# A transformer block on one core: the attention's residual moves from VectorE to TensorE and ScalarE

## The chip, the cores and the metric

The kernel runs on one core of a Trainium2 chip. The metric is the device time of one execution in microseconds (us), as the median of several runs. All five engines of the core work side by side, each through its own list of instructions in the order in which they are written; semaphores join them.

## The reference, cut to what matters

The input x has the shape (2, 128 channels, 128, 128). Two residual blocks follow each other.

```python
x = x + attention(ln_c(x))        # shifted 8x8 windows, 8 heads, then a 128x128 projection Wproj and bproj
t = tokens(x)                     # 32768 tokens of 128 channels
t = t + ffn(ln_t(t))              # graph attention over 524288 edges gives gates for 4 experts
```

Inside the attention the last two steps are `einsum('oc,bchw->bohw', Wproj, out) + bproj`, and then the sum with the x that came in. That sum with x, the first residual, is what the change moves. Everything is float32. The graph part needs the edges sorted by their destination.

## The kernel before

**Stages.** The program has three stages. The first (to about 1937 us) computes the attention and, on VectorE in the time that is left there, sorts the 524288 edges with a network of compare-and-exchange steps. The second (to about 7400 us) gathers rows for the sorted edges with GpSimd's indirect DMAs, while the experts are computed. The third joins the gates and the experts. The change is in the first stage.

**Strips and rounds.** The image is cut into 32 strips of 8 rows (1024 tokens, 16 windows). A loop of 34 rounds runs a pipeline over them: round t normalizes strip t (`has_m`), makes scores and exponentials of strip t-1 (`has_n`), and weighs, projects, adds the residual to and normalizes strip t-2 (`has_c`). So the residual is added in rounds 2 to 33, once per strip, in two halves j of 4 rows (512 tokens) each.

**Banks.** PSUM's banks 6 and 7 are used by turns: use u of a round lies in bank 6 + u % 2. TensorE raises `full[u % 2]` when a use is written, and the engine that copies it out raises `evac[u % 2]`; `free(u)` makes TensorE wait for the copy of the use before. Uses 6 and 7 are the two halves of the projection, uses 8 and 9 the centering of the sum x1 for the second normalization.

**The order on each engine in one round**, as far as it touches the change, with the lines of the profile:

- VectorE (`round_dve`): weigh window group 0 (L648); add biases and take maxima for the scores of group 0 (L628, L636, L639); a slot of sort steps (L420, L421); weigh group 1 (L648), which completes `ot`; a slot of sort steps; **the residual, four `scalar_tensor_tensor` (L665, L667)**; the scores of group 1 (L628, L633, L636, L639); two more slots of sort steps.
- TensorE (`round_pe`): attend to group 0 (L769, L785, L791), scores of group 0 (L805), center x (L746), attend to group 1, two means (L750), **the projection, halves 0 and 1 (L841)**, the scores of group 1 (L805), the centering of x1 (L746), values (L864), two means (L750), queries and keys (L884), the node rows (L895).
- ScalarE (`round_act`): copies of PSUM for the attention (L926), inverse sums (L934, L936), exponentials (L963), the log and inverse square root of the variance (L950, L956), the square and copy of the centered x1 (L942, L943), the values (L996), log and inverse root again, queries and keys (L1010 to L1016), exponentials (L963), node rows (L1026).
- SyncE stores x1, x2 and the node rows of a strip, and loads the strip after next but one into the same `xt` when uses 6 and 7 have been copied out.

The projection needs both weighed groups: TensorE waits with the second mean and the projection until VectorE has written `ot` for group 1. The scores of group 1 on VectorE need TensorE's L805 for group 1, which stands behind the projection in TensorE's list.

**The sort and its turns.** From round 8 on, each level of the sort takes three rounds. The steps across partitions need the keys turned by TensorE. In the first round of a level (8, 11, ... 29; called A here) VectorE asks for a turn after its third slot, and TensorE turns 8 pieces at the end of its round (L715), with ScalarE copying them out (L910). In the second round (9, 12, ... 30; B) VectorE asks for the turn back after its second slot, and TensorE turns 8 pieces between the values, after it centered x1 (L715, L907). In the third round (10, 13, ... 31; C) there is no turn. Rounds 2 to 7 have only sort steps, and rounds 32 and 33 end the pipeline. A constant `ident`, the 128x128 identity that the transposes use as well, lies in SBUF.

Of the kernel before, what the change touches and what calls it, by code (L numbers as in the profile page):

```python
# [11 lines left out]
ALU = mybir.AluOpType  # L12
ACT = mybir.ActivationFunctionType
# [4 lines left out]
IMGS, H, W = 2, 128, 128  # L18
M = IMGS * H * W
NH, DK, WS, SS = 8, 16, 8, 4  # L20
# [126 lines left out]
OPEN = 4  # L147
# [16 lines left out]
def program(nc, x, wq_t, bq, wkv_t, bkv, wproj_t, bproj, bias_table, w_gat, att_src, att_dst, b_gat, ln_gamma,  # L164
# [9 lines left out]
    with ExitStack() as ctx:  # L174
        scopes = [ctx]

        def sb(name, shape, dt=F32):
            return scopes[-1].enter_context(nc.sbuf_tensor(name, shape, dt))

        def sem(name):  # L180
            return ctx.enter_context(nc.semaphore(name))

        bank = ctx.enter_context(nc.psum_tensor("bank", [P, 8, 512], F32))
        cst = sb("cst", [P, CONST_COLS])

        def con(name):
            return cst[:, CONST[name][0]:CONST[name][1]]
# [4 lines left out]
        vec = sb("vec", [C, 9])  # L192
# [19 lines left out]
        evac = [sem(f"evac{b}") for b in range(2)]  # L212
        full = [sem(f"full{b}") for b in range(2)]
# [11 lines left out]
        strip_saved = sem("strip_saved")  # L225
# [71 lines left out]
        bias = sb("bias", [P, 4, NH // 2, L])  # L297
# [20 lines left out]
        xt = [a.rearrange("c (i w) -> c i w", w=W) for a in parts[:UNROLL]]  # L318
# [11 lines left out]
        x1 = [sb(f"x1{b}", [C, WS, W]) for b in range(UNROLL)]  # L330
# [270 lines left out]
        def pass_over(e, semaphore, before, n):  # L601

            e.wait_ge(semaphore, before + OPEN)
            e.sem_inc(semaphore, n)

        def has(t):

            return 0 <= t < STRIPS, 0 <= t - 1 < STRIPS, 0 <= t - 2 < STRIPS

        def round_dve(e, t, d, own):  # L610
            _, has_n, has_c = has(t)
            par = (t - 2) % UNROLL

            def scores(g):
                if not has_n:
                    pass_over(e, biased, t * 3 + g, 1 + g)
                    pass_over(e, centered, t * 2 + g, 1)
                    return
                e.wait_ge(s_full, t * 2 + g + 1 + OPEN)

                e.wait_ge(pt_full[1], pt_uses(t, g, 1) + 2 + OPEN)
                kind = 2 * ((t - 1) % 16 // 15)

                sums = bank[:, 0:4, :].rearrange("p (a b) (w x) -> p a (b w) x", a=2, w=4)
                taken = prob[g][:, :, :, :].rearrange("p w (a b) s -> p a w (b s)", a=2)
                biases = bias[:, :].rearrange("p k (a b) s -> p a k (b s)", a=2)
                n = 8 - g
                e.tensor_tensor(taken[:, :, 0:n], sums[:, :, 0:n],  # L628
                                biases[:, :, kind:kind + 1].broadcast_to([P, 2, n, 2 * L]),
                                ALU.add).then_inc(biased, 1)  # L630
                if g:

                    e.tensor_tensor(taken[:, :, n:8], sums[:, :, n:8], biases[:, :, kind + 1:kind + 2],  # L633
                                    ALU.add).then_inc(biased, 1)
                e.wait_ge(biased, t * 3 + 1 + 2 * g + OPEN)
                own.step(e.tensor_reduce(row_max[:, g], prob[g][:, :, :, :], AX, ALU.max))  # L636
                own.settle()
                pr = prob[g][:, :, :, :].rearrange("p w h s -> p (w h) s")
                e.tensor_tensor(pr, pr, row_max[:, g].rearrange("p w h -> p (w h)").unsqueeze(2)  # L639
                                .broadcast_to([P, 32, L]), ALU.subtract).then_inc(centered, 1)  # L640

            def weigh_attention(g, u):
                if not has_c:
                    return

                wait_full(e, t, u)
                e.wait_ge(sums_turned, t * 2 + g + 1 + OPEN)
                e.tensor_tensor(ot[:, 8 * g:8 * g + 8].rearrange("p w i j -> p (w i j)"), bank[:, 6 + u % 2, :],  # L648
                                inv[g][:, :], ALU.mult).then_inc(evac[u % 2], 1)

            weigh_attention(0, 0)
            scores(0)
            if t:
                sort_slot(d, t, 0)
            weigh_attention(1, 3)
            sort_slot(d, t, 1)
            if has_c:
                for j in range(2):

                    wait_full(e, t, 6 + j)  # L660
                    e.wait_ge(strip_saved, t - 3 + OPEN)
                    pr = bank[:, 6 + j, :].rearrange("p (i c) -> p i c", c=W)
                    rws = slice(4 * j, 4 * j + 4)
                    old = xt[par]
                    e.scalar_tensor_tensor(x1[par][:, rws, SS:W], pr[:, :, 0:W - SS], vec[:, 6:7],  # L665
                                           old[:, rws, SS:W], ALU.add, ALU.add)
                    e.scalar_tensor_tensor(x1[par][:, rws, 0:SS], pr[:, :, W - SS:W], vec[:, 6:7],  # L667
                                           old[:, rws, 0:SS], ALU.add, ALU.add).then_inc(evac[j], 1)
            scores(1)
            sort_slot(d, t, 2)  # L670
            sort_slot(d, t, 3)


        def pt_uses(t, g, b):

            each = 3 - b
            return t * (2 * each) + each * g

        def wait_evac(e, t, u):
            e.wait_ge(evac[u % 2], t * USES + u // 2 + 1 + OPEN)  # L680

        def wait_full(e, t, u):
            e.wait_ge(full[u % 2], t * USES + u // 2 + 1 + OPEN)
# [41 lines left out]
        def round_pe(e, t, k, strips, loads, turns=0, across=None, back=None):  # L725
# [3 lines left out]
            has_m, has_n, has_c = strips  # L729
            now, before, last = k, (k - 1) % UNROLL, (k - 2) % UNROLL  # L730

            def free(u):

                e.wait_ge(evac[u % 2], t * USES + u // 2 + OPEN)

            def skip(u):

                free(u)
                e.sem_inc(full[u % 2], 1)
                e.sem_inc(evac[u % 2], 1)  # L740

            def bk(u):
                return bank[:, 6 + u % 2, :]
# [90 lines left out]
            for j in range(2):  # L834
                if has_c:
                    if j == 0:

                        wait_evac(e, t, 0)
                        wait_evac(e, t, 3)
                    free(6 + j)  # L840
                    e.matmul(bk(6 + j), wproj_s[:, :],  # L841
                             ot[:, :, 4 * j:4 * j + 4, :].rearrange("c w i j -> c i w j"),
                             start=True, stop=True).then_inc(full[j], 1)
                else:
                    skip(6 + j)
            score(1)
# [7 lines left out]
            for g in range(2):  # L854
                if has_n:
                    free(10 + g)
                    for w in range(8):
# [4 lines left out]
                        for half in range(2):  # L862
# [3 lines left out]
                                         start=True, stop=True)  # L866
# [12 lines left out]
            for g in range(2):  # L879
                for n, wgt in enumerate((wq_s[:, :], wkv_s[:, 0:C])):  # L880
                    u = 14 + 2 * g + n
                    if has_m:
                        free(u)
                        e.matmul(bk(u), wgt, xw[now][:, 8 * g:8 * g + 8].rearrange("c w i j -> c (w i j)"),  # L884
                                 start=True, stop=True).then_inc(full[n], 1)
# [4 lines left out]
            for j in range(2):  # L890
                if has_c:
                    e.wait_ge(xn_done, t * 4 + 3 + j + OPEN)
                    free(18 + j)
                    for r in range(4):
                        m = e.matmul(bank[:, 6 + j, ROW * r:ROW * r + ROW], x2[last][:, 4 * j + r, :], wgat_s[:, :],  # L895
                                     start=True, stop=True)
# [19 lines left out]
        def round_act(e, t, k, strips, turns=0, across=False, back=False):  # L916
            has_m, has_n, has_c = strips
            last = (k - 2) % UNROLL
# [19 lines left out]
            def centered_copy(n, u0):  # L938
                for j in range(2):
                    u = u0 + j  # L940
                    wait_full(e, t, u)
                    e.activation(sq[n][:, j], bank[:, 6 + u % 2, :], ACT.Square)  # L942
                    e.activation(xc[n][:, j], bank[:, 6 + u % 2, :], ACT.Copy).then_inc(evac[u % 2], 1)  # L943
# [34 lines left out]
            else:  # L978
                pass_over(e, rstd_ready, t * 4, 2)
            if has_c:  # L980

                e.wait_ge(xn_done, t * 4 + OPEN)
                centered_copy(1, 8)
            if has_n:
                for g in range(2):
# [3 lines left out]
                    for half in range(2):  # L989

                        rws = slice(64 * half, 64 * half + 64)
# [610 lines left out]
        def _(e):  # L1602
# [11 lines left out]
            for t in range(ROUNDS):  # L1614
                round_dve(e, t, d, own)
# [29 lines left out]
        def _(e):  # L1645
# [3 lines left out]
            for t in range(FIRST_ALL):  # L1649
                if t == 1:  # L1650

                    e.wait_ge(setup_done, 1)
                round_pe(e, t, t, has(t), 1)
            with e.Fori(0, (FIRST_TURN - FIRST_ALL) // UNROLL) as i:
                for k in range(FIRST_ALL, FIRST_ALL + UNROLL):
                    round_pe(e, i * UNROLL + k, k % UNROLL, (True,) * 3, i + k // UNROLL + 1)
            with e.Fori(0, LEVELS // 2) as i:
                for level in range(2):
                    turns = i * 4 + 2 * level

                    for k, keyed in enumerate((dict(across=key(0)), dict(back=key(1 - level)), {})):
                        t = FIRST_TURN + UNROLL * level + k
                        round_pe(e, i * (2 * UNROLL) + t, t % UNROLL, (True,) * 3, i * 2 + t // UNROLL + 1,
                                 turns + k, **keyed)
# [286 lines left out]
```

## Time and profile before

| | |
|---|---|
| median of 3 runs | 8058.88 us (8057.36 to 8060.34) |
| the profiled execution, its own time | 8058.64 us |
| its span in the profile | 8056.8 us |
| busy in the span: TensorE, VectorE, ScalarE, GpSimd | 3009.5, 3627.7, 1934.5, 4712.0 us |
| mean granted TensorE clock | 0.666 |

A share of busy time over the whole span says little here, since the stages have different limits: in the second stage GpSimd is busy three quarters of the time, in the first VectorE and TensorE about four fifths each. The change has to be judged inside the first stage, by what each engine waits for in a round. A line like `L841 MATMUL ... x4` stands for two float32 matmuls: the chip's list has two passes for each, and each pass has a weight load of its own.

### The profile page before, as it was taken

Reading aid. Unit: us, or ns where it says so; the run is one execution under the profiler, and the core shown is the slowest. Engines: PE = TensorE matmul, PEld = TensorE weight load, DVE = VectorE, ACT = ScalarE, POOL = GpSimd, SP = SyncE. Lnnn points to the kernel's source line nnn. Section 1 sums busy time; section 2 is a strip of 40 time slices with the busy share of each in tenths; the row PEclk is TensorE's granted clock in tenths of the full one; section 3 lists DMA queues with packets and bytes.
Section 4 is the critical chain, followed back from the end, with each engine's and each line's share of the span. In section 5 each row is a group of like instructions: output and inputs, shape, how many; then the busy total and the mean of one; then the engine's idle time right before and its main releaser. Section 6 shows DMA issues by size and latency. Waiting matters only on the chain.

```text
span 8056.8 us, 48889 instructions
## 1 busy us (share of the span) xinstructions
PE 3009.5 (37%) x14746; PEld 1474.1 (18%) x14746; DVE 3627.7 (45%) x3863; ACT 1934.5 (24%) x2929; POOL 4712.0 (58%) x4876
## 2 busy tenths in 40 slices
PE   3678887775122222222222212221212121200678
PEld 2345544442000100000001100000000000000222
DVE  5997788885323332333233324321211111111799
ACT  1446665552112121212121212121111111100000
POOL 1111121114777777777777777777777777776641
PEclk9889999897565666666666656665656565655555
DMA  1001111011122222222222222221111111111455
GB/s 52 26 26 34 34 34 34 29 32 57 45 70 57 70 65 62 57 70 69 58 57 70 71 56 57 70 54 31 41 31 41 31 41 31 39 18 46 137 184 173
DMA packets 284782, 455.39 MB, mean 57 GB/s; under 512 B 121214, under 2 KB 204382, under 8 KB 262366
## 3 DMA queue, kind: packets, MB, share of 16 engines
q1 hardware_dynamic: 134760, 395.08, 13.4%
q0 software_dynamic: 147648, 56.99, 6.4%
q8 instruction: 111, 1.82, 0.1%
q10 hardware_dynamic: 2208, 1.05, 0.1%
q14 instruction: 55, 0.45, 0.0%
HBM read 231.36 MB, written 221.42 MB: 56 GB/s over the span
## 4 chain that ended last, share of the span: by engine, by line
POOL 52%; issue 20%; DVE 3%; PE 1%; DMA 1%; POOLq 0%; ACT 0%; DVEq 0%
POOL gath L1319 51%; PE bank L1561 1%; DVE yo L1534 1%; POOL got L1596 1%; DMA gate_rows<-gate_dram 0%; DMA gate_dram<-turned_gates 0%; DVE fin L1539 0%; DVE s L1495 0%; DVE sc L1470 0%; POOL first L1749 0%; DVE s L1468 0%; DMA got<-edge_rows,end_i 0%; DVE sc L1482 0%; DVE sc L1489 0%; DVE sc L1474 0%
## 5 line engine op out<-in xcount | busy, mean ns | idle before, releaser
L1319 POOL DMA_INDIRECT gath<-node_rows,idx x4352 | 4125.3, 948 | 1326.3 <-issue 1326.3
L1272 PE MATMUL bank<-xm,w_s 128*128 128x512 f32 x1024 | 640.7, 770 | 3744.5 <-ACT scratch_i L1293 3732.3
L1228 DVE TENSOR_TENSOR adst_in<-bank,gath 128x256 f32<-128x256 f32 x68 | 53.4, 786 | 2819.5 <-DMA gath<-node_rows,idx 2819.5
L1272 PEld LDWEIGHTS bank<-xm,w_s 128*128 128x128 f32 x1024 | 227.4, 241 | 4142.8 <-ACT scratch_i L1293 3999.3
L1300 ACT ACTIVATE bank<-diff 128x256 f32<-128x256 f32 x68 | 26.3, 387 | 3740.4 <-DVE diff L1245 3740.4
L1046 POOL TENSOR_TENSOR scratch_i<-xc,dst_f 128x480 f32<-128x480 f32 x64 | 121.1, 1892 | 1128.6 <-ACT dst_f L956 1128.6
L1279 PE MATMUL bank<-scratch_i,w_s 128*128 128x512 f32 x1024 | 540.1, 685 | 195.7 <-ACT scratch_i L1293 118.5
L1215 DVE TENSOR_SCALAR scratch_i<-bank,b_s 128x512 f32<-128x512 f32 x256 | 190.4, 750 | 917.6 <-PE bank L1279 522.4
L1561 PE MATMUL bank<-gate_rows,choose 4*128 4x512 f32 x512 | 447.4, 1065 | 62.1 <-DVE yo L1534 50.5
L1293 ACT ACTIVATE scratch_i<-bank,b_s 128x512 f32<-128x512 f32 x512 | 345.1, 683 | 187.6 <-PE bank L1272 186.8
L1596 POOL DMA_INDIRECT got<-edge_rows,end_i x256 | 245.3, 958 | 208.3 <-DVE gates L1522 130.6
L1057 POOL TENSOR_TENSOR x<-xc,dst_f 128x512 f32<-128x512 f32 x64 | 159.5, 2510 | 354.0 <-ACT dst_f L956 354.0
L1310 ACT ACTIVATE rows<-sums 128x1280 f32<-128x1280 f32 x68 | 230.4, 3388 | 390.2 <-DVE sums L1256 390.2
L1279 PEld LDWEIGHTS bank<-scratch_i,w_s 128*128 128x128 f32 x1024 | 217.4, 220 | 522.2 <-issue 420.2
L1539 DVE TENSOR_REDUCE fin<-yo 128x512 f32<-128x2560 f32 x64 | 288.0, 4500 | 4.3
L420 DVE TENSOR_TENSOR key_a<-key_b 128x1024 f32<-128x1024 f32 (+1 forms) x144 | 266.6, 1852 | 2.3
L421 DVE TENSOR_TENSOR key_b<-key_a 128x1024 f32<-128x1024 f32 (+1 forms) x139 | 258.3, 1858 | 0.0
L420 DVE TENSOR_TENSOR key_b<-key_a 128x1024 f32<-128x1024 f32 (+1 forms) x139 | 244.7, 1760 | 29.4 <-ACT key_a L907 27.3
L421 DVE TENSOR_TENSOR key_a<-key_b 128x1024 f32<-128x1024 f32 (+1 forms) x144 | 253.3, 1759 | 0.0
L1561 PEld LDWEIGHTS bank<-gate_rows,choose 4*128 4x128 f32 x512 | 163.8, 328 | 335.4 <-issue 233.6
L791 PE MATMUL bank<-pt,vb 128*64 128x64 f32 x4096 | 210.5, 250 | 31.7 <-ACT pt L926 31.0
L1250 DVE TENSOR_TENSOR terms<-bank,gath 128x1024 f32<-128x1024 f32 x68 | 182.2, 2679 | 63.5 <-ACT weight L1302 63.5
(216 smaller groups left out, 5650.0 us busy)
## 6 DMA issues: line engine op xcount, KB each, us to landing
gath<-node_rows,idx POOLq DMA_INDIRECT x4352
y_dram<-scratch_i SPq DMA_DIRECT2D x64, 1024.0 KB, 4.0
yo<-y_dram SPq DMA_DIRECT2D x64, 1024.0 KB, 5.1
edge_rows<-rows SPq DMA_DIRECT2D x68, 768.0 KB, 3.3
line<-moved SPq DMA_DIRECT2D x21, 2048.0 KB, 7.2
moved<-line SPq DMA_DIRECT2D x20, 2048.0 KB
scratch_i<-in_x SPq DMA_DIRECT2D x64, 256.0 KB, 2.7
x_dram<-x SPq DMA_DIRECT2D x64, 256.0 KB, 2.1
```

The lines of the kernel that those rows point to most:

```text
L420: d.step(e.tensor_tensor(small, lower, upper, ALU.min))
L421: d.step(e.tensor_tensor(large, lower, upper, ALU.max))
L791: m = e.matmul(bank[64 * hh:64 * hh + 64, 6 + u % 2, L * w:L * w + L], vb[:, 8 * g + w, hh, v, :], pt[:, w, hh, 64 * v:64 * v + 64], start ...
L1215: e.tensor_scalar(yt[par][:, ex, :], bank[:, 2 + b, :], b2_s[:, ex:ex + 1], None, ALU.add).then_inc(y_evac[b], 1)
L1272: e.matmul(bank[:, k % 2, :], w1_s[:, k // 2, P * (k % 2):P * (k % 2) + P], xm[par][:, :], start=True, stop=True).then_inc(up_full, 1)
L1279: m = e.matmul(bank[:, 2 + b, :], w2_s[:, ex, k, :], hid[:, 2 * ex + k, :], start=k == 0, stop=k == 1)
L1293: e.activation(hid[:, k, :], bank[:, k % 2, :], ACT.Gelu, bias=b1_s[:, k // 2, k % 2:k % 2 + 1]).then_inc(hidden, 1)
L1310: e.activation(rw[:, 0:20], sums[:, :, :, 1:].rearrange("p q h j -> p (q h) j"), ACT.Copy)
L1319: e.indirect_dma_start(gath[par][:, j, :], None, node_rows, bass.IndirectOffsetOnAxis(ap=idx[par][:, j:j + 1].bitcast(U32), axis=0)).then_ ...
L1539: e.tensor_reduce(fin[b][:, :], yo[b][:, :, :].rearrange("c e t -> c t e"), AX, ALU.add).then_inc(fin_ready, 1)
L1561: m = e.matmul(bank[:, 4 * (k % 2) + ex, :], choose[:, ex, :], gate_rows[par][:, 4 * k:4 * k + 4, :].rearrange("e b t -> e (b t)"), start= ...
L1596: e.indirect_dma_start(got[par][:, j, :], None, edge_rows, bass.IndirectOffsetOnAxis(ap=end_i[:, 32 * g + j:32 * g + j + 1].bitcast(U32), ...
```

## The change

The four VectorE instructions of the residual are taken out. TensorE adds the old x onto the projection in PSUM: each half gets two more float32 matmuls with the identity as weights, one over 496 columns and one over 16 (4 rows of 124 and of 4, since the strip is rolled by 4 columns against its windows). ScalarE copies the sum out with the bias of the projection, in two ACTIVATEs per half, and raises `evac` in VectorE's stead. In ScalarE's list these four stand right ahead of the squares of the centered x1.

```diff
 def round_dve
             sort_slot(d, t, 1)
-            if has_c:
-                for j in range(2):
-                    wait_full(e, t, 6 + j)
-                    e.wait_ge(strip_saved, t - 3 + OPEN)
-                    pr = bank[:, 6 + j, :].rearrange("p (i c) -> p i c", c=W)
-                    rws = slice(4 * j, 4 * j + 4)
-                    old = xt[par]
-                    e.scalar_tensor_tensor(x1[par][:, rws, SS:W], pr[:, :, 0:W - SS], vec[:, 6:7],
-                                           old[:, rws, SS:W], ALU.add, ALU.add)
-                    e.scalar_tensor_tensor(x1[par][:, rws, 0:SS], pr[:, :, W - SS:W], vec[:, 6:7],
-                                           old[:, rws, 0:SS], ALU.add, ALU.add).then_inc(evac[j], 1)
             scores(1)
 def round_pe
                     e.matmul(bk(6 + j), wproj_s[:, :],
                              ot[:, :, 4 * j:4 * j + 4, :].rearrange("c w i j -> c i w j"),
-                             start=True, stop=True).then_inc(full[j], 1)
+                             start=True, stop=False)
+                    pr = bk(6 + j).rearrange("p (i c) -> p i c", c=W)
+                    old = xt[last][:, 4 * j:4 * j + 4, :]
+                    e.matmul(pr[:, :, 0:W - SS], con("ident"), old[:, :, SS:W], start=False, stop=False)
+                    e.matmul(pr[:, :, W - SS:W], con("ident"), old[:, :, 0:SS],
+                             start=False, stop=True).then_inc(full[j], 1)
 def round_act
             if has_c:
+                for j in range(2):
+                    wait_full(e, t, 6 + j)
+                    e.wait_ge(strip_saved, t - 3 + OPEN)
+                    pr = bank[:, 6 + j, :].rearrange("p (i c) -> p i c", c=W)
+                    rws = slice(4 * j, 4 * j + 4)
+                    e.activation(x1[last][:, rws, SS:W], pr[:, :, 0:W - SS], ACT.Identity, bias=vec[:, 6:7])
+                    e.activation(x1[last][:, rws, 0:SS], pr[:, :, W - SS:W], ACT.Identity,
+                                 bias=vec[:, 6:7]).then_inc(evac[j], 1)
                 e.wait_ge(xn_done, t * 4 + OPEN)
                 centered_copy(1, 8)
```

## Rows read from the trace of the kernel before

**Rows 1.** Busy time by engine in a stretch: PE, PEld, DVE, ACT, POOL; granted clock; DMA.

```profile
700.00:1000.00 300.00, 245.53 (x2190) 152.91 (x2189) 238.16 (x147) 182.76 (x314) 57.40 (x48) 0.93 0.11 35
```

**Rows 2.** Who waited for whom, 400 to 1500 us: total us, times, longest.

```profile
DVE ot L648 <- ACT inv L936: 77.7, 13, 10.8
...
PE bank L750 <- DVE ot L648: 53.0, 21, 6.7
...
DVE prob L628 <- PE bank L805: 12.5, 20, 1.4
...
PE bank L746 <- DVE x L667: 6.2, 2, 5.5
```

**Rows 3.** Timeline of VectorE in round 16 (a C round): start, duration.

```profile
1010.23 0.68 DVE L648 TENSOR_TENSOR ot<-bank,inv 128x512 f32<-128x512 f32 x1
...
1015.23 0.73 DVE L665 SCALAR_TENSOR_TENSOR x<-bank,vec,scratch_i 128x496 f32<-128x496 f32 x1
...
1016.80 2.01 DVE L628 TENSOR_TENSOR prob<-bank,bias 128x1792 f32<-128x1792 f32 x1
```

**Rows 4.** Timeline of TensorE in round 16.

```profile
1011.05 1.10 PE L750 MATMUL bank<-dst_f,cst 128*128 128x512 f32 x2 [1.67 <-DVE ot L648]
1011.99 2.07 PE L841 MATMUL bank<-ot,wproj_s 128*128 128x512 f32 x4
1013.99 2.06 PE L805 MATMUL bank<-k,q 64*128 64x128 f32 x32
1016.15 1.98 PE L746 MATMUL bank<-x,cst 128*128 128x512 f32 x4
```

**Rows 5.** Timeline of ScalarE in round 16: its idle time around the projection.

```profile
1012.77 1.14 ACT L956 ACTIVATE dst_f<-dst_f 128x512 f32<-128x512 f32 x2
1017.31 0.60 ACT L942 ACTIVATE dst_f<-bank 128x512 f32<-128x512 f32 x1 [3.40 <-PE bank L746]
```

**Rows 6.** Timeline of VectorE in round 15 (a B round) and into round 16.

```profile
965.04 2.02 DVE L628 TENSOR_TENSOR prob<-bank,bias 128x1792 f32<-128x1792 f32 x1 [1.11 <-PE bank L805]
...
997.84 0.69 DVE L648 TENSOR_TENSOR ot<-bank,inv 128x512 f32<-128x512 f32 x1 [10.80 <-ACT inv L936]
```

**Rows 7.** Timeline of TensorE in round 15.

```profile
962.93 2.06 PE L805 MATMUL bank<-k,q 64*128 64x128 f32 x32
964.92 1.98 PE L746 MATMUL bank<-x,cst 128*128 128x512 f32 x4
```

**Rows 8.** Timeline of VectorE, rounds 3, 5, 14, 30 and after 33.

```profile
321.15 2.01 DVE L628 TENSOR_TENSOR prob<-bank,bias 128x1792 f32<-128x1792 f32 x1
...
435.58 2.02 DVE L628 TENSOR_TENSOR prob<-bank,bias 128x1792 f32<-128x1792 f32 x1 [1.12 <-PE bank L805]
...
891.74 0.69 DVE L648 TENSOR_TENSOR ot<-bank,inv 128x512 f32<-128x512 f32 x1 [1.09 <-ACT inv L936]
...
1766.61 0.15 DVE L547 COPY sign_now<-cst 128x1 f32<-128x1 f32 x1
...
1919.37 0.29 DVE L420 TENSOR_TENSOR tail_a<-tail_b 128x128 f32<-128x128 f32 x1 [12.40 <-ACT tail_b L914]
```

**Rows 9.** Timeline of TensorE, rounds 18, 30 and 32.

```profile
1116.33 1.98 PE L746 MATMUL bank<-x,cst 128*128 128x512 f32 x4 [0.63 <-DVE x L667]
...
1767.90 3.68 PE L746 MATMUL bank<-x,cst 128*128 128x512 f32 x4 [6.94 <-DVE x L667]
1771.41 0.60 PE L715 MATMUL bank<-cst,key_a 128*128 128x128 f32 x4
...
1859.90 3.58 PE L841 MATMUL bank<-ot,wproj_s 128*128 128x512 f32 x4 [3.31 <-PEq L740]
```

**Rows 10.** Groups by line and form, 400 to 1500 us: busy us, mean ns of one.

```profile
L769 PE MATMUL bank<-cst,prob 128*128 128x128 f32 x667 | 121.2, 325 | 23.7 <-ACT node L1026 17.6 <-issue 6.1
...
L895 PE MATMUL bank<-wgat_s,x 128*128 128x24 f32 x336 | 45.4, 277 | 8.5 <-ACT k L1016 5.4 <-ACT q L1011 3.2
...
L1010 ACT ACTIVATE q<-bank,vec,cst 128x512 f32<-128x512 f32 x42 | 32.7, 778 | 0.0
```

**Rows 11.** The chain that ended last, in order of time, where the first stage ends.

```profile
1936.97 6.48 POOL first L1749
```

## The prediction, made before the changed kernel was run

> **What bounds the kernel now.** The chain that ended last shows that everything behind 1937 us hangs on the first stage: GpSimd's first gather starts there [rows 11], released by the end of the sort, and the sort's last steps waited 12.40 us for TensorE's last turn at the end of round 33 [rows 8]. So a microsecond added to or saved on the chain of rounds moves the end by a microsecond, and the stages behind it are left as they are.
>
> Inside the stage two engines are full: in 700 to 1000 us TensorE is busy 245.5 and VectorE 238.2 of 300 us, ScalarE 182.8 [rows 1]. Which of the two sets the time is read from the waits [rows 2], and it alternates. VectorE waits for `inv`, the end of attention on TensorE and ScalarE, 77.7 us; TensorE waits for VectorE's `ot` 53.0 us. The timelines show where. In C and A rounds VectorE runs without a gap through its sort steps, and TensorE stands still until `ot` comes (1.67 us in round 16 [rows 4]). From the turn at the end of A through B to the next C, TensorE and ScalarE set the time: VectorE waits 10.80 us for `inv` at the head of round 16 [rows 6].
>
> The place of the change is short. When `ot` is there, TensorE runs the second mean, the projection, the scores of group 1, the centering. VectorE meanwhile does one slot of sort steps, the residual (1015.23 to 1016.80, 1.57 us [rows 3]), and then wants the scores of group 1. TensorE ended these at 1013.99 + 2.06 = 1016.05 [rows 4], so they were 0.75 us early; with the 0.05 us that a wait takes to end (in round 15 the matmuls end at 964.99 and L628 starts at 965.04 [rows 6, 7]) TensorE has **0.7 us to spare** in such a round, less than the residual takes.
>
> **What the change removes and adds.** VectorE loses 1.57 us per strip, 32 times. TensorE gains, per strip, four passes of 496 columns and four of 16, each with its weight load. The projection's four passes of 512 columns take 2.00 us from start to the next group's start [rows 4], 0.50 each; 496 columns give 0.484, four of them 1.94 us. For 16 columns the nearest row is L895, 24 columns with a weight load for every pass: 45.4 us / 336 = 0.135 us [rows 10], which holds some time at the lower clock; I take 0.115, and 0.46 for four. So **c = 2.4 us** more on TensorE per strip. Bounds from rows: 1.94 if the narrow passes vanish behind the wide ones, 3.0 if each takes the full 0.277 us that a single L895 lasts [rows 10] (1.94 + 1.11). The lower end needs weight loads that are wholly hidden, and L895 shows that between narrow passes they aren't, so I stay near the row.
>
> The Trainium skill weighs this otherwise: its page "TensorE: Matmul & The Clock Gate", section "Back-to-back issue gap", gives about 25 ns as the gap of an isolated matmul with 1 to 64 columns at the full clock. By that four narrow passes would be 0.1 us, c about 2.04, and the sum below some 10 us smaller (an estimate from that page). L895's 135 ns speaks against it, since each pass there brings its own weights, as here.
>
> ScalarE gains four ACTIVATEs. The nearest row with a bias is L1010, 0.778 us for 512 columns [rows 10]; even at that price for both pieces a half costs 1.56 us. Half 0 is copied while TensorE projects half 1, and half 1 while it computes the scores of group 1 (2.06 us [rows 4]), before the centering needs it. ScalarE has ended L956 by 1013.91 and idles 3.40 us until L942 [rows 5]; the copies fall into that time and delay nothing else on ScalarE. I put them at nothing; if the cover were gone (a copy of over 2 us) the centering would come later by the excess. The wait for `strip_saved` moves from VectorE's list to ScalarE's; it concerns strip t-3's store, a round back. Behind it stand the squares, which need the centering anyway. SyncE's loads wait on the same `evac`, half a microsecond to two later, and are wanted more than half a round afterwards.
>
> **Round by round.** The scores of group 1 come c later after `ot`, VectorE asks for them 1.57 us earlier. I went through all 32 rounds on VectorE's timeline:
>
> - *TensorE sets the time, +c.* 16 rounds. In six B rounds (9, 12, 15, 21, 24, 27) VectorE already waits for the scores, or stands just at that limit, and the centering follows them at once [rows 6, 7], so all that hangs on TensorE moves by c. In rounds 2, 5, 6, 7 and 23 VectorE waited 0.56 to 1.40 us there (round 5 [rows 8]). In 32 and 33 TensorE runs alone to the end. Rounds 13, 19 and 25 are C rounds whose successor begins with a wait of 1.09 to 1.58 us for `inv` (round 14 [rows 8]), so TensorE's path counts. 16 x 2.4 = +38.4.
> - *VectorE sets the time, +(c - 0.7).* 11 A and C rounds like round 16 (10, 11, 14, 16, 17, 20, 22, 26, 28, 29, 31), all with 6.57 us from L648 to L628 [rows 3]. What VectorE saves is turned into a wait for the scores. 11 x 1.7 = +18.7.
> - *The slot is longer, -1.57.* In rounds 3, 4 and 8 the slot has twice the steps, and the scores are ready long before (round 3 has no wait [rows 8]). 3 x 1.57 = -4.7.
> - *Round 18*: centering waited 0.63 us for VectorE's x1 [rows 9]; ScalarE gives it earlier. 2.4 - 0.6 = +1.8.
> - *Round 30*: the slot holds a long copy, and centering waited 6.94 us for x1 [rows 9]. Now it is done before the turn is asked for (1766.61 + 0.15 [rows 8]), so the turn starts at about 1766.9 and not at 1771.41 [rows 9]: -4.5.
>
> Sum: 38.4 + 18.7 - 4.7 + 1.8 - 4.5 = **+49.7 us**, or 28 x c - 17.5. On the profiled execution's 8058.6 us that is 8108; it lies 0.2 us from the median of the runs, so nothing is corrected. With c at its bounds the sum is +36.8 (8095) and +66.5 (8125).
>
> **The rivals.**
>
> *VectorE's saving reaches the end (faster).* Place: the A and C rounds, where VectorE has no gap. For it: VectorE is what TensorE waits for there (53.0 us [rows 2]). It needs TensorE's added passes to fit into the spare. Decision point: 28 x c = 17.5, c = 0.63 us per strip; with passes at nothing the sum is -17.5, 8041. Against it: c would have to be a quarter of what four 512-column passes cost in the same place, and the passes stand behind the wait for `ot`, not inside it.
>
> *Identity passes are cheap (about the same).* The transposes L769 also multiply by `ident` and take one pass per 128 columns where the projection takes two per matmul, 121.2 / 667 = 0.18 us [rows 10]. If the added matmuls took one pass each, c = 2 x 0.484 + 2 x 0.115 = 1.2, the sum +16, 8075. Against it: the centering L746 has weights from the same constant tile and lists two passes for each matmul [rows 7].
>
> *The clock gives something back.* In ten rounds TensorE starts the projection at the lower of its two clocks after idle time before `ot`, as in round 32, 3.58 us for the passes that otherwise take 2.07 [rows 9, 4]; the mean granted clock of a middle stretch is 0.93 [rows 1]. With the mean ahead of it such starts cost some 16 us. If denser work kept the clock at 2.4 GHz there, the sum would be +34, 8092. The Trainium skill's "TensorE: Matmul & The Clock Gate", section "Why this matters for your kernels", advises to leave no gaps between bursts, which would be the reason. Against it: the idle time lies ahead of `ot`, and the change puts its work behind it.
>
> *ScalarE's copies are late.* They stand in ScalarE's list behind the inverse roots of uses 4 and 5, and ahead of the squares. If the centering waited one more microsecond in the 16 rounds that TensorE sets, the sum were +66, and with c at 3.0 over +80, 8140.
>
> **How the numbers follow.** My forecast (c from 1.94 to 3.0 in this sum) has 0.68; the clock 0.10; cheap passes 0.10; VectorE's saving reaching the end 0.06; late copies or dearer passes 0.06. A change of under 0.2% (16 us) can't be told from none in this kernel. Cheap passes lie on that bound and are split, a little under half to slower: same 0.07, faster 0.06, slower 0.87. The range goes from 8076 (cheap passes are cut, the clock is taken in) to 8128 (just over the dear end).
>
> **What would show it.** Right: L841 and the added matmuls together about 4.4 us from the projection's start to the scores'; L628 of group 1 waiting for L805 in all but some four rounds, 1.7 us later after L648 in A and C rounds; VectorE's busy time 50 us less, TensorE's 75 us more; the period of three rounds (about 150 us) 5 to 6 us longer; GpSimd's first gather at about 1987 us, and all behind it the same. Wrong: if the added passes start at 1 us together; if the first gather moves by less than 16 us; if the centering waits for ScalarE; or if TensorE's wait for `ot` shrinks by what it gained.

## The result: 38.6 us slower, and the profile after

The changed kernel takes 8097.65 us (median of 5 runs, 8096.24 to 8099.73), against 8059.05 (5 runs, 8057.36 to 8060.34) for the kernel before: ratio 1.0048 [1.0034, 1.0063], slower by 38.6 us. The forecast was 8108, 10 us more; its range (8076 to 8128) holds the time. The profiled execution took 8097.65 us with a span of 8095.8. In its trace L738 is the mean, L829 the projection, L834 and L835 the added matmuls, L793 the scores, L734 the centering, L979 and L980 ScalarE's copies, L943 and L949 the log and inverse root, L935 and L936 square and copy, L757 and L779 the attention's transposes and values, L703 the turn. The experiments' line numbers are shifted by a few; the operands tell the instruction there (`ot,wproj_s` is the projection, `scratch_i,cst` with 496 or 16 columns the identity).

Busy time of the whole span, on the page:

```profile
PE 3069.7 (38%) x15002; PEld 1522.9 (19%) x15002; DVE 3578.2 (44%) x3735; ACT 1988.3 (25%) x3057; POOL 4707.3 (58%) x4876
```

VectorE has 49.5 us less and TensorE 60.2 more (1.88 per strip; the forecast had 75). The place of the change on TensorE in round 16, on its timeline (start, duration; answers to [rows 4]):

```profile
1025.63 1.10 PE L738 MATMUL bank<-dst_f,cst 128*128 128x512 f32 x2 [1.68 <-DVE ot L648]
1026.56 1.02 PE L829 MATMUL bank<-ot,wproj_s 128*128 128x512 f32 x2
1027.42 1.00 PE L834 MATMUL bank<-scratch_i,cst 128*128 128x496 f32 x2
1028.25 0.29 PE L835 MATMUL bank<-scratch_i,cst 128*128 128x16 f32 x2
1028.39 1.10 PE L829 MATMUL bank<-ot,wproj_s 128*128 128x512 f32 x2
1029.33 1.00 PE L834 MATMUL bank<-scratch_i,cst 128*128 128x496 f32 x2
1030.17 0.29 PE L835 MATMUL bank<-scratch_i,cst 128*128 128x16 f32 x2
1030.39 2.06 PE L793 MATMUL bank<-k,q 64*128 64x128 f32 x32
1032.37 1.99 PE L734 MATMUL bank<-x,cst 128*128 128x512 f32 x4
```

The wait for `ot` is what it was (1.68 against 1.67 us), and all that is new stands behind it. From the projection's start to the scores' it is 3.83 us against 2.00 [rows 4]: **c is 1.83 us**, where the forecast had 2.4. VectorE in the same round, on its timeline (answers to [rows 3]):

```profile
1024.80 0.69 DVE L648 TENSOR_TENSOR ot<-bank,inv 128x512 f32<-128x512 f32 x1
...
1032.49 2.02 DVE L628 TENSOR_TENSOR prob<-bank,bias 128x1792 f32<-128x1792 f32 x1 [2.61 <-PE bank L793]
```

The residual is gone, and in its place stands a wait of 2.61 us for the scores. L628 comes 7.69 us after L648 instead of 6.57: 1.12 later, which is c less the 0.7 us that TensorE had to spare. The table of waits, 400 to 1500 us (total, times, longest; answers to [rows 2]), shows the same over many rounds:

```profile
DVE prob L628 <- PE bank L793: 77.8, 32, 7.6
...
PE bank L738 <- DVE ot L648: 44.8, 18, 6.2
```

VectorE's wait for scores has grown from 12.5 us to 77.8, while TensorE's wait for `ot` has shrunk only from 53.0 to 44.8: the passes don't fill it. ScalarE's new copies, on its timeline in round 16 (answers to [rows 5]):

```profile
1028.66 0.67 ACT L979 ACTIVATE x<-bank,vec 128x496 f32<-128x496 f32 x1 [0.17 <-PE bank L835]
1029.23 0.27 ACT L980 ACTIVATE x<-bank,vec 128x16 f32<-128x16 f32 x1
1030.49 0.68 ACT L979 ACTIVATE x<-bank,vec 128x496 f32<-128x496 f32 x1 [1.00 <-PE bank L835]
1031.07 0.27 ACT L980 ACTIVATE x<-bank,vec 128x16 f32<-128x16 f32 x1
1033.53 0.60 ACT L935 ACTIVATE dst_f<-bank 128x512 f32<-128x512 f32 x1 [2.20 <-PE bank L734]
```

They end at 1031.34, a microsecond before the centering starts on TensorE (1032.37), and ScalarE still idles 2.20 us behind them. In the chain that ended last the first stage ends here (answers to [rows 11]):

```profile
1978.70 6.48 POOL first L1750
```

The first gather comes 41.7 us later than in the kernel before (forecast 50). The rest of the program takes 2.7 less, so that the span is 39.0 longer; the five runs of the changed kernel differ by more than that (3.5 us).

### The profile page after: what moved, and what is told of

Read it like the earlier page. It is cut to its first block, busy times and chain, and to the rows that moved or that the text cites. A ratio compares the mean times of both kernels' runs of the same rounds, so it can differ in the third digit from the quotient of the medians.

```text
span 8095.8 us, 49431 instructions
## 1 busy us (share of the span) xinstructions
PE 3069.7 (38%) x15002; PEld 1522.9 (19%) x15002; DVE 3578.2 (44%) x3735; ACT 1988.3 (25%) x3057; POOL 4707.3 (58%) x4876
## 3 DMA queue, kind: packets, MB, share of 16 engines
q8 instruction: 115, 1.88, 0.1%
## 4 chain that ended last, share of the span: by engine, by line
POOL 51%; issue 20%; DVE 3%; PE 2%; DMA 0%; POOLq 0%; ACT 0%; DVEq 0%
POOL gath L1320 51%; PE bank L1562 2%; DVE yo L1535 1%; POOL got L1597 1%; DVE fin L1540 0%; DMA gate_rows<-gate_dram 0%; DMA gate_dram<-turned_gates 0%; DVE s L1496 0%; DVE sc L1471 0%; POOL first L1750 0%; DVE s L1469 0%; DVE sc L1475 0%; DVE sc L1490 0%; DVE sc L1481 0%; DVE sc L1483 0%
## 5 line engine op out<-in xcount | busy, mean ns | idle before, releaser
L420 DVE TENSOR_TENSOR key_b<-key_a 128x1024 f32<-128x1024 f32 (+1 forms) x139 | 245.0, 1762 | 29.9 <-ACT key_a L900 27.8
L779 PE MATMUL bank<-pt,vb 128*64 128x64 f32 x4096 | 208.0, 248 | 29.2 <-ACT pt L919 28.0
L757 PE MATMUL bank<-cst,prob 128*128 128x128 f32 x1024 | 198.2, 341 | 47.2 <-ACT node L1027 28.5
```

Source lines behind the costliest of these rows:

```text
L420: d.step(e.tensor_tensor(small, lower, upper, ALU.min))
L757: m = e.transpose(bank[:, 4 + b, P * (2 * w + hh):P * (2 * w + hh) + P], prob[g][:, 2 * wp + w, 2 * hh:2 * hh + 2, :] .rearrange("p k s -> ...
L779: m = e.matmul(bank[64 * hh:64 * hh + 64, 6 + u % 2, L * w:L * w + L], vb[:, 8 * g + w, hh, v, :], pt[:, w, hh, 64 * v:64 * v + 64], start ...
```

## The experiments

The first four ran on one chip, where the kernel before took 8061.95 us (21 runs); the last three on another, with 8054.14 (13 runs). Each ratio is to the kernel before on the same chip. "First gather" is GpSimd's L1745 to L1754 in the one execution that was profiled; it starts at 1936.97 us in the kernel before and at 1978.70 in the changed one, and what is said of it compares with these two traces, whatever the chip. Costs and gains "by rounds" are differences to the kernel before in the distance from one round's first L648 to the next round's.

**The copies without the passes.** The changed kernel without the four identity matmuls per strip:

```diff
-                             start=True, stop=False)
-                    e.matmul(pr[:, :, 0:W - SS], con("ident"), old[:, :, SS:W], ...)
-                    e.matmul(pr[:, :, W - SS:W], con("ident"), old[:, :, 0:SS], ...)
+                             start=True, stop=True).then_inc(full[j], 1)
```

> The changed kernel without TensorE's identity matmuls (the residual x is left out of x1); ScalarE still copies the projection out with the bias, VectorE still has no residual. Theory (TensorE's added passes behind ot are the whole loss): VectorE's saving is kept and nothing is paid for, 28 x 0 - 17.5, so about 8041 us, 8035 to 8048. Rival (ScalarE's copies and the later hand-over of x1 cost the time): not faster than before, 8059 us or more.

Measured: 8051.17 us, ratio 0.9988 [0.9979, 0.9998], above the expected 8035 to 8048; first gather at 1926.57, 10.4 us earlier than before. So VectorE's work does move the end, but by 10.4 us and not by 17.5. By rounds, rounds 3 and 4 bring 6.4 of it, and the eleven A and C rounds, which have 7.7 us in the 17.5, bring 1.6. Rounds 16 and 17 on VectorE's timeline show where the rest stays:

```profile
1002.88 0.69 DVE L648 TENSOR_TENSOR ot<-bank,inv 128x512 f32<-128x512 f32 x1
...
1008.74 2.02 DVE L628 TENSOR_TENSOR prob<-bank,bias 128x1792 f32<-128x1792 f32 x1 [0.78 <-PE bank L793]
...
1036.84 0.69 DVE L648 TENSOR_TENSOR ot<-bank,inv 128x512 f32<-128x512 f32 x1 [1.09 <-ACT inv L924]
```

L628 comes 0.71 us earlier after L648, as expected, but the next round then begins with a wait of 1.09 us for `inv`, which the kernel before and the changed one don't have there. In the kernel before `inv` was ready 1.57 us ahead of this L648 (L936 ended at 1042.14, L648 started at 1043.71), more than the 0.71 us. The view by windows (length, busy time of TensorE, its loads, VectorE, ScalarE and GpSimd, granted clock as a share of TensorE's full 2.4 GHz, DMA share, GB/s) from L628 to the next L648, first here:

```profile
1008.74:1036.84 28.10, 23.80 (x200) 15.07 (x202) 26.84 (x13) 18.02 (x33) 7.17 (x8) 0.82 0.20 62
```

then in the changed kernel:

```profile
1032.49:1059.42 26.93, 22.55 (x216) 14.03 (x216) 26.76 (x13) 18.02 (x33) 5.34 (x4) 0.94 0.21 64
```

The granted clock is 0.82 against 0.94 (0.94 too in the kernel before). TensorE's attention ran longer at the lower level of 1.2 GHz, as in these two lines of its timeline here

```profile
1031.35 1.12 PE L757 MATMUL bank<-cst,prob 128*128 128x128 f32 x4
1032.40 1.18 PE L779 MATMUL bank<-pt,vb 128*64 128x64 f32 x16
```

beside the same two in the changed kernel:

```profile
1053.74 0.66 PE L757 MATMUL bank<-cst,prob 128*128 128x128 f32 x4
1054.32 0.73 PE L779 MATMUL bank<-pt,vb 128*64 128x64 f32 x16
```

In rounds 16, 22 and 28 this run gains nothing (it loses 0.46 to 0.48 us in each); in round 31, where VectorE meets no such wait, it keeps the whole 0.71.

**The passes without the copies.** The kernel before with the identity matmuls added, VectorE's residual kept:

```diff
-                             start=True, stop=True).then_inc(full[j], 1)
+                             start=True, stop=False)
+                    e.matmul(pr[:, :, 0:W - SS], con("ident"), old[:, :, SS:W], ...)
+                    e.matmul(pr[:, :, W - SS:W], con("ident"), old[:, :, 0:SS], ...).then_inc(full[j], 1)
```

> The kernel before with TensorE's identity matmuls added and VectorE's residual kept (x is added twice). Theory: c = 1.83 us counts in 16 rounds, 1.13 in the 11 A and C rounds, about 1.2 in round 18, and nothing is saved in rounds 3, 4, 8 and 30: +43, about 8102 us, 8098 to 8108, so VectorE's removal brought the changed kernel only some 5 us. Rival (VectorE's 1.57 us per strip were saved on the path): 8097.6 + 50 = 8148 us. Rival (ScalarE's copies cost the time): close to before, under 8070 us.

Measured: 8112.45 us, ratio 1.0064 [1.0047, 1.0080], some 4 us over the expected range; first gather 51.3 us later, in the chain that ended last:

```profile
1988.31 6.48 POOL first L1754
```

The expectation had +43. By rounds the excess stands in round 8 (3.3 us, expected 0), in 11, 17 and 29 (2.7 to 2.9, expected 1.13) and in 18 (2.3, expected 1.2). With the run before, the change is taken apart into two parts that add up: the passes +51.3, the move off VectorE -10.4, together +40.9, and both at once +41.7.

**The identity first.** The changed kernel with the identity matmuls ahead of the second mean, that is ahead of the wait for `ot`, into PSUM banks 4 and 5, onto which the projection is then added:

```diff
             for j in range(2):
+                if j == 1 and has_c:
+                    for h in range(2):
+                        e.wait_ge(pt_evac[1 - h], ...)
+                        e.matmul(pr[:, :, 0:W - SS], con("ident"), old[:, :, SS:W], start=True, stop=False)
+                        e.matmul(pr[:, :, W - SS:W], con("ident"), old[:, :, 0:SS], start=False, stop=False)
                 (second mean)
-                    e.matmul(bk(6 + j), wproj_s[:, :], ot..., start=True, stop=False)
+                    e.matmul(bank[:, 5 - j, :], wproj_s[:, :], ot..., start=False, stop=True)
```

Left out above: `free(6 + j)` and the identity matmuls behind the projection go, and ScalarE copies from banks 5 and 4.

> The changed kernel with the identity matmuls ahead of the second mean, in the time in which TensorE waits for ot, into banks 4 and 5, and the projection accumulated onto them there. Theory: the idle 1.7 to 2.4 us ahead of ot take up the 1.83 us, behind ot nothing is added, so the loss goes and a part of VectorE's saving is kept: 8033 to 8050 us. Rival (the loss comes from more TensorE work in a stage in which TensorE is full, wherever it stands): still 8085 us or more.

Measured: 8043.01 us, ratio 0.9970 [0.9952, 0.9987], within the expected range; first gather at 1918.22. TensorE in round 16, timeline:

```profile
1001.97 0.99 PE L820 MATMUL bank<-scratch_i,cst 128*128 128x496 f32 x2
1002.80 0.29 PE L821 MATMUL bank<-scratch_i,cst 128*128 128x16 f32 x2
1002.94 1.08 PE L820 MATMUL bank<-scratch_i,cst 128*128 128x496 f32 x2
1003.85 0.29 PE L821 MATMUL bank<-scratch_i,cst 128*128 128x16 f32 x2
1003.99 1.10 PE L738 MATMUL bank<-dst_f,cst 128*128 128x512 f32 x2
1004.93 1.88 PE L835 MATMUL bank<-ot,wproj_s 128*128 128x512 f32 x4
1006.75 2.06 PE L793 MATMUL bank<-k,q 64*128 64x128 f32 x32
```

The same eight passes now fill the time in which TensorE waited for `ot`; in this round that wait is gone, and over the kernel the loss is gone. The place of the passes in the list made the change slower, not their number.

This run also ends below the one without any passes (8051.17 us, same chip), and their runs don't overlap: 8040.58 to 8045.59 against 8048.11 to 8056.06. Round 21 on TensorE's timeline, without the passes

```profile
1258.50 1.53 PE L738 MATMUL bank<-dst_f,cst 128*128 128x512 f32 x2 [2.53 <-DVE ot L648]
1259.82 3.18 PE L829 MATMUL bank<-ot,wproj_s 128*128 128x512 f32 x4
```

and with the passes ahead of the wait:

```profile
1258.53 1.10 PE L738 MATMUL bank<-dst_f,cst 128*128 128x512 f32 x2 [0.52 <-DVE ot L648]
1259.46 1.88 PE L835 MATMUL bank<-ot,wproj_s 128*128 128x512 f32 x4
```

After 2.53 us of idle time the projection ran at the lower level; with the passes in that time it ran at the full one, and the round took 49.75 us instead of 52.19, at a granted clock of 0.97 instead of 0.90. The banks differ too, so what the clock alone brings isn't isolated.

**The scores first.** The changed kernel with the scores of group 1 ahead of the second mean, the identity left where the change put it:

```diff
             for j in range(2):
+                if j == 1:
+                    score(1)
                 (means)
...
                 (projection and identity)
-            score(1)
```

> The changed kernel with TensorE's scores of group 1 ahead of the second mean, so that they don't stand behind the projection and the identity matmuls. Theory: VectorE no longer waits for them in A and C rounds and keeps its 1.57 us there, and TensorE's idle time ahead of ot takes the scores' 2.0 us, which makes up for the added passes in B rounds: 8018 to 8040 us. Rival (TensorE full): 8085 us or more.

Measured: 8032.59 us, ratio 0.9964 [0.9952, 0.9977], within the expected range; first gather at 1907.10. VectorE, timeline of round 16:

```profile
992.46 0.69 DVE L648 TENSOR_TENSOR ot<-bank,inv 128x512 f32<-128x512 f32 x1
...
997.46 2.02 DVE L628 TENSOR_TENSOR prob<-bank,bias 128x1792 f32<-128x1792 f32 x1
```

L628 follows L648 after 5.00 us, 1.57 less than in [rows 3], with no wait: up to there the whole residual is saved. The distance to the next round isn't shorter for it, since VectorE then waits 1.74 us for `inv` at the head of round 17; of the 29.9 us by which the first gather comes earlier, 16.8 stand in rounds 2 to 7. So the time came in part from other rounds than the A and C rounds of the expectation. TensorE in round 16:

```profile
991.54 2.06 PE L793 MATMUL bank<-k,q 64*128 64x128 f32 x32
993.53 1.13 PE L738 MATMUL bank<-dst_f,cst 128*128 128x512 f32 x2
994.49 1.02 PE L831 MATMUL bank<-ot,wproj_s 128*128 128x512 f32 x2
...
998.24 2.21 PE L734 MATMUL bank<-x,cst 128*128 128x512 f32 x4
```

The scores stand in the time before `ot`, and the centering starts 5.78 us after L648, with the passes in between; in the kernel before it was 1016.15 - 1010.23 = 5.92 [rows 3, 4].

**The scores first, in the kernel before.** The same edit of the order, with the residual left on VectorE, to see what the order alone is worth.

> The kernel before, with only TensorE's scores of group 1 moved ahead of the second mean; the residual stays on VectorE. Theory: the order of TensorE's list is a gain by itself, since the 1.7 to 2.4 us of idle time ahead of ot take up the scores in the rounds that TensorE sets: 8035 to 8052 us. Rival (only the moved residual makes this order pay): within 5 us of before.

Measured: 8045.10 us, ratio 0.9987 [0.9978, 0.9997], within the expected range; first gather at 1931.26. TensorE now waits for VectorE's x1 ahead of the centering, timeline of round 16:

```profile
1011.02 1.98 PE L746 MATMUL bank<-x,cst 128*128 128x512 f32 x4 [1.83 <-DVE x L667]
```

So with this order the moved residual pays (0.9987 to 0.9964, intervals that don't touch, each to its own chip's kernel before), while with the old order it costs 0.48%.

**Both first.** The scores and then the identity ahead of the second mean, the two edits above together.

> The changed kernel with both the scores of group 1 and the identity matmuls ahead of the second mean: 3.9 us of work for 1.7 to 2.4 us of idle time. Theory (what fits into the idle time is free, what goes over is paid again): not better than the scores alone by more than 5 us, 8022 to 8040 us. Rival (all that stands ahead of ot is free): 8010 us or less.

Measured: 8021.31 us, ratio 0.9958 [0.9941, 0.9975], just below the expected 8022 to 8040; first gather at 1899.27. The lowest ratio of the study, but its interval overlaps that of the scores alone, so nothing beyond the scores is shown. Of the 37.7 us at the first gather the end doesn't get all: the rest of the program took 6126 us in this trace, against 6115 in the two other runs of this chip; why stays open. TensorE, timeline of round 16:

```profile
1002.45 1.98 PE L734 MATMUL bank<-x,cst 128*128 128x512 f32 x4 [0.83 <-ACT x L982]
```

Here the cover of ScalarE's copies is gone, since the scores no longer stand between the projection and the centering: TensorE waits 0.83 us for them. From 400 to 1500 us it does so 19 times, 15.1 us in all.

**The identity twice.** The changed kernel with each pair of identity matmuls issued twice, to price a strip's passes a second time where no spare is left:

```diff
+                    e.matmul(pr[:, :, W - SS:W], con("ident"), old[:, :, 0:SS], start=False, stop=False)
+                    e.matmul(pr[:, :, 0:W - SS], con("ident"), old[:, :, SS:W], start=False, stop=False)
```

> The changed kernel with the identity matmuls issued twice (x is added twice), 3.66 us per strip. Theory (added passes behind ot are paid for in nearly every strip): from no passes (e1) to one set the time rose by 46 to 49 us, so by as much again: 8143 to 8150 us. Rival (the clock gives denser work a part back, or TensorE's idle time takes up a second set): under 8130 us.

Measured: 8157.20 us, ratio 1.0125 [1.0108, 1.0142], above what was expected; first gather at 2040.00, 61.3 us after the changed kernel's. Round 16 on TensorE and on VectorE, timelines:

```profile
1051.55 1.02 PE L829 MATMUL bank<-ot,wproj_s 128*128 128x512 f32 x2
...
1057.49 2.06 PE L793 MATMUL bank<-k,q 64*128 64x128 f32 x32
```

```profile
1059.59 2.02 DVE L628 TENSOR_TENSOR prob<-bank,bias 128x1792 f32<-128x1792 f32 x1 [4.72 <-PE bank L793]
```

5.94 us from the projection to the scores, 2.11 more than with one set. 61.3 / 2.11 is 29 strips' worth: with the spare used up nearly every strip pays in full. The granted clock from 235 us to the first gather is 0.90 here and in the changed kernel, so denser work behind `ot` gave nothing back that shows.

## Why the prediction was right, and where its sizes were off

**The mechanism held; that the time came within 11 us is in part luck,** since two errors of opposite sign meet below. The passes stand behind `ot` in TensorE's list, the scores of group 1 come later, and VectorE's saving turns into a wait for them (12.5 us to 77.8). Doing either part alone, and moving either the passes or the scores ahead of the wait, shows it: all three ways that take the passes from between `ot` and the scores (leaving them out, the identity first, the scores first) end below the kernel before.

**ScalarE's copies at nothing: right.** 0.67 + 0.27 us a half stay under the 2.06 us of the scores. The run with both first shows the price when that cover is gone, 0.83 us in round 16 there.

**The term that was mis-sized is c, 2.4 us for the passes of a strip.** It measured 1.83. Three parts, all in round 16. The four wide passes take 0.83 + 0.84 = 1.67 us, not 1.94. The four narrow ones take 0.14 + 0.22 = 0.36, not 0.46. And the projection's own halves shrink from 2.00 to 0.86 + 0.94 = 1.80; that is a part of the first error too, since the 0.50 us per pass was read from a group with a wait inside. In the kernel before, TensorE's weight load for half 1 waited for ScalarE to copy out the mean that lay in its bank, on the timeline of the loads in round 16:

```profile
1012.93 0.30 PEld L841 LDWEIGHTS bank<-ot,wproj_s 128*128 128x128 f32 x2 [0.75 <-ACT dst_f L950]
```

Half 0's two passes start 0.43 us apart. About 0.2 us of the 2.00 was that wait, and in the changed kernel half 0's identity passes fill it; in the run with the identity first, where the projection goes to other banks and has no such wait, its four passes take 1.82 us from their start to the scores'. With c = 1.83 the forecast's 28 c - 17.5 is +33.7 us. (28 x 1.83 = 51.2 meets the +51.3 of the passes alone by chance: with the residual still on VectorE the forecast's rule has c - 0.7 in the A and C rounds, and the expectation was +43.) The Trainium skill's page "TensorE: Matmul & The Clock Gate", section "Back-to-back issue gap", by whose 25 ns the estimate of c was 2.04, came nearer than the forecast's 2.4; but that figure is for an isolated matmul, and the narrow passes here, each with its own weight load, measured 0.09 us on average. So c fell below both estimates mainly through the wide passes and the hidden wait.

**The second term, -17.5, was too large for what the move brings alone:** -10.4. In the run with the copies alone rounds 3 and 4 brought more than -1.57 each (-3.2), but round 30 only -1.7 instead of -4.5, round 8 nothing, and the eleven A and C rounds together -1.6 instead of -7.7: in rounds 16, 22 and 28 the 0.7 us were lost again behind L628, at the lower clock. The forecast took it that in these rounds what VectorE saves stays saved.

**By rounds**, as the distance between the first L648 of one round and of the next: the A and C rounds like 16 were to cost c - 0.7, which is 1.13 with the measured c. Rounds 10, 16, 22, 28 and 31 cost 1.12 to 1.30. Six rounds (8, 17, 18, 24, 29, 30) came out 10.6 us above the rule with c = 1.83, and the others 2.6 below it. In four of the six (17, 18, 24, 29) TensorE spent longer at the lower clock than in the kernel before, as in round 17 of the changed kernel, timeline of TensorE:

```profile
1072.10 1.10 PE L738 MATMUL bank<-dst_f,cst 128*128 128x512 f32 x2 [2.12 <-ACT dst_f L943]
1073.03 1.88 PE L829 MATMUL bank<-ot,wproj_s 128*128 128x512 f32 x2
1074.70 1.86 PE L834 MATMUL bank<-scratch_i,cst 128*128 128x496 f32 x2
...
1076.55 1.10 PE L829 MATMUL bank<-ot,wproj_s 128*128 128x512 f32 x2
```

Half 0 and its identity take 3.52 us, half 1 and its own 2.00. Round 17 costs 2.82 and round 29 costs 2.79 in the same way, and the run with the passes alone repeats both (2.75 and 2.78). In round 30 the centering did come before the turn, as forecast, and the turn started 0.2 us behind VectorE's L547 instead of 4.7; but from L628 to the end of the round the granted clock was 0.84 instead of 0.90, and the round came out only 1.8 us shorter. What each of these shifts would be without the clock was not tried, and the net of +8 us over all rounds (41.7 - 33.7) is read from rows, not isolated; its cause stays open. It happens to make up half of the 16 us that c was too dear: the forecast was near because a too dear pass and a missing term had opposite signs.

**The rivals.** VectorE's saving reaching the end: not in the changed kernel; without the passes 10.4 us of it do. One pass per matmul: refuted, two are listed and priced. The clock giving something back: not with the passes behind `ot`, where eleven rounds still start the projection at the lower level (ten before) and the granted clock from 235 us to the first gather is 0.90 against 0.89. With the passes ahead of `ot`, in the idle time itself, round 21 above shows it; that the idle time lies ahead of `ot` and the passes behind it is what the prediction held against this rival. Late copies: only with the scores moved away.

## What to carry to other kernels

Work that is added to an engine costs by where it stands in that engine's list: put what doesn't need the late operand ahead of the wait for it. The same move made this kernel 0.48% slower with its eight passes behind the wait, 0.30% faster with them ahead of it, and 0.42% faster with the scores ahead as well; with the passes in the idle time it was even faster than without them. Time freed on one engine is worth what its next wait lets through, so look for that wait before counting the saving; and read the price of an instruction from starts inside a group that holds no wait, the engine's weight loads included.

## What the hardware showed unexpectedly

In these rows the level of the clock after a short idle time was not to be told from its length. In round 17 of the changed kernel TensorE idled 2.12 us before the second mean and then ran half 0 at the lower level; in the kernel before it had idled 2.39 us at the same place and the projection ran at the full one:

```profile
1056.39 1.10 PE L750 MATMUL bank<-dst_f,cst 128*128 128x512 f32 x2 [2.39 <-DVE ot L648]
1057.33 2.07 PE L841 MATMUL bank<-ot,wproj_s 128*128 128x512 f32 x4
```

And in the run with the copies alone round 16, whose scores VectorE took 0.71 us earlier, ran from there on at a granted 0.82 instead of 0.94 and the distance to the next round came out 0.48 us longer than in the kernel before. What decides the level there stays open.
